# Products without a reader in the idle stretches of TensorE, first and last tile of an audio tower block

## The chip, the cores and the metric

The kernel runs on one core of one Trainium2 chip. The metric is the device time of one execution in microseconds, given as the median of the runs.

## The reference

The input x is 64 samples of 96 channels and 512 positions, fp32. First comes a small attention on each sample ("token attention"), then one transformer block (grouped attention, then a gated feed-forward with ternary weights) over the 64 x 32 rows of 512 that result:

```python
def reference(x, Wq, Wk, Wv, Wo, qn_w, kn_w, w1, w2, w3):
    q, k, v = split(x, 3, axis=1)                        # 64 x 32 x 512 each
    h = einsum('bts,bcs->bct', softmax(q^T k * scale), v)
    # attention of 16 query heads and 4 key/value heads of 128; rows of one sample
    # (32) attend to each other, causal; q and k are RMS-normed and rotated
    h = h + attn(layernorm(h), Wq, Wk, Wv, qn_w, kn_w) @ Wo.T
    y = layernorm(h)
    return h + (sigmoid(y @ Q(w1).T) * (y @ Q(w2).T)) @ Q(w3).T   # Q rounds to -1, 0, 1; 1408 hidden
```

## The kernel before

The program has two stages. `token_attention` computes the first attention and, beside it, prepares the weights in SBUF (fp16 high and low halves of the attention weights, `W.hi` and `W.lo`, and the ternary feed-forward weights). It ends near 390 us, and a barrier separates it from the second stage. `blocks`, the second stage, is the one that the diff touches.

`blocks` works on 16 tiles of 128 rows (`NTT`). Each engine has its own instruction stream, written out by hand; `over_tiles` gives it as `body(0)` (attention of tile 0 alone), a loop over tiles 1 to 14, `body(15)`, and `body(16)`, in which only the feed-forward of tile 15 is left. The loop body works on the attention of tile n and the feed-forward of tile n - 1 together. Engines wait for each other by semaphores that count upwards.

TensorE (the engine of the diff) issues in this order within a body:

- `project(n, c)` for c = 1 to 5 (lines 991 to 993): four column groups of Q, and V. The one of K, `project(n + 1, 0)`, is issued ahead, in the body before. Each has 12 products of 128x128 weights with 512 columns in fp16 (high x high, high x low, low x high, four slices of the depth). `project(n, 0)` waits for the transposed normalised rows `x_hi`, `x_lo`, which arrive by a DMA from what ScalarE and GpSimd write.
- `gate_products` (lines 1033, 1034) of the tile before: three groups (`FG`) by two halves, 176 products of 128 columns in all. The first waits for the second normalisation's rows, again by a transposing DMA.
- between them `transpose_qk` for c = 0 to 4 (line 985), at places that `TRANSPOSE_AT` lists. Each waits for `q_ready`, GpSimd's last step of the rotation and normalisation of that head group (`rope_sum`, lines 722, 725, 729). Then come the `scores` (line 1051, 32 small products), which wait for ScalarE's copies.
- `down_products` 0 to 3 (lines 1068, 1069), `project(n + 1, 0)`, `weigh_values` (line 1082, waits for the softmax that VectorE finishes in line 952), `down_products` 4 to 10, and `output_products` (lines 1096 to 1098, 48 products of 512 columns), which wait for the high and low halves of the context (`ctx_hi` by ScalarE, `ctx_lo` by VectorE, line 891).

In tile 0 there is no feed-forward, so TensorE has no gate and down products between the steps of the attention; in `body(15)` there is no next projection, and in `body(16)` nothing is left between the output products and the gate products but the second normalisation.

The eight PSUM banks are `PROJ[0..1]`, `TR[0..1]` and `FB[0..3]`. `FB[1..3]` hold projections or gate sums, and all four `FB` hold the context; `PROJ[1]` takes the output sum; `TR[0]` takes transposes and the down sum.

Of the kernel before, what the change touches and what calls it, by code (L numbers as in the profile page):

```python
# [16 lines left out]
P = 128  # L17
# [10 lines left out]
D = 512  # L28
# [3 lines left out]
Q_AT, K_AT, V_AT, O_AT = 0, KD * HEADS * HD, KD * (HEADS + KV) * HD, KD * (HEADS + 2 * KV) * HD  # L32
# [536 lines left out]
def blocks(nc, W, h1, tables_in, norm_in, mask_in, ident_in, out):  # L569

    with ExitStack() as ctx:
# [6 lines left out]
        PROJ = [ctx.enter_context(nc.psum_tensor(f"proj{n}", [P, D], FP32)) for n in range(2)]  # L578
        TR = [ctx.enter_context(nc.psum_tensor(f"transposed{n}", [P, D], FP32)) for n in range(2)]
        FB = [ctx.enter_context(nc.psum_tensor(f"ffn_sum{n}", [P, D], FP32)) for n in range(BT)]  # L580
# [70 lines left out]
        SCORES_AT = (1, 1)  # L651
        BANK = (PROJ[0], FB[2], FB[3], PROJ[0], PROJ[1], TR[1])
        DOWN_FIRST = 4
        block = ctx.enter_context(nc.Block())

        def over_tiles(eng, body):
# [322 lines left out]
        def _(pe):  # L979
            pe.wait_ge(const_in, 4 * DMA)  # L980

            def transpose(dst, src, last_sem):

                for k in range(KD):
                    t = nc.tensor.transpose(dst[:, k * P:(k + 1) * P], src[:, k * P:(k + 1) * P], ident[:, :])  # L985
                t.then_inc(last_sem, 1)

            def split_products(dst, pairs, done):

                for i, (ah, al, bh, bl) in enumerate(pairs):  # L990
                    nc.tensor.matmul(dst, ah, bh, start=(i == 0), stop=False)  # L991
                    nc.tensor.matmul(dst, ah, bl, start=False, stop=False)  # L992
                    t = nc.tensor.matmul(dst, al, bh, start=False, stop=(i == len(pairs) - 1))  # L993
                t.then_inc(done, 1)

            def project(n, c):

                if c == 0:
                    pe.wait_ge(x_turned, 2 * DMA * (n + 1))
                first = isinstance(n, int) and n == 0  # L1000
                if c == 0 and not first:
                    pe.wait_ge(squared, 5 * n - 1)
                    pe.wait_ge(roped_b, 5 * n - 1)
                if c == 3:
                    pe.wait_ge(squared, 5 * n + 1)
                    pe.wait_ge(roped_b, 5 * n + 1)
                if c in (1, 2) and not first:
                    pe.wait_ge(c_lo, BT * n)
                if c == 4 and not first:
                    pe.wait_ge(h2_done, n)  # L1010
                if c == NPROJ - 1 and not first:
                    pe.wait_ge(taken, n)
                pairs = []
                for k in range(KD):
                    at = (K_AT + k * KV * HD if c == 0 else V_AT + k * KV * HD if c == NPROJ - 1
                          else Q_AT + k * HEADS * HD + (c - 1) * D)
                    pairs.append((xh[:, k, :], xl[:, k, :], W.hi(at, D), W.lo(at, D)))
                split_products(BANK[c][:, :], pairs, proj)

            def gate_products(n, f, m):  # L1020

                if f == 0 and m == 0:
                    pe.wait_ge(x2_turned, 2 * DMA * (n + 1))
                    pe.wait_ge(c_hi, KV * (n + 1))
                    pe.wait_ge(c_lo, KV * (n + 1))
                if f == 2:
                    pe.wait_ge(gated, NF * n + 1 + START)
                for j, t in enumerate(FG[f]):
                    for k in range(KD):
                        at = (m * KD + k) * FF + t * P  # L1030
                        w = ffn_w[:, at:at + P]
                        dst = FB[2 * (f % 2) + m][:, j * P:(j + 1) * P]
                        nc.tensor.matmul(dst, w, x2h[:, k, :], start=(k == 0), stop=False)  # L1033
                        ins = nc.tensor.matmul(dst, w, x2l[:, k, :], start=False, stop=(k == KD - 1))  # L1034
                ins.then_inc(f1, 1)

            def transpose_qk(n, c, ffn):
                pe.wait_ge(q_ready, 5 * n + c + 1)
                if c == 0 and ffn:
                    pe.wait_ge(o_out, n - 1 + START)  # L1040
                if c == 1:
                    pe.wait_ge(v_out, n + 1)
                if c >= 2:
                    pe.wait_ge(qkt_out, 5 * n + c - 1)
                transpose(TR[c % 2], rope[:, c, :], qkt)

            def scores(n):
                pe.wait_ge(qkt_out, 5 * n + 5)
                for h in range(KV):
                    for b in range(BT):  # L1050
                        ins = nc.tensor.matmul(SCORES[b * SEQ:(b + 1) * SEQ, h * P:(h + 1) * P],
                                               kT[:, h, b * SEQ:(b + 1) * SEQ], qT[:, h, b * P:(b + 1) * P],
                                               start=True, stop=True)
                ins.then_inc(scored, 1)

            def down_products(n, tiles):
                if tiles[0] == 0:
                    if isinstance(n, int) and n + 1 >= NTT:
                        pe.wait_ge(o_out, n + START)
                    else:  # L1060
                        pe.wait_ge(qkt_out, 5 * (n + 1) + 5)
                for k in tiles:
                    if k == 0 or k in (FG[1][0], FG[2][0]):
                        f = [g[0] for g in FG].index(k)
                        pe.wait_ge(hid_hi, NF * n + f + 1)
                        pe.wait_ge(hid_lo, NF * n + f + 1)
                    at = 2 * KD * FF + k * D
                    nc.tensor.matmul(DOWN[:, :], hh[:, k, :], ffn_w[:, at:at + D], start=(k == 0), stop=False)
                    ins = nc.tensor.matmul(DOWN[:, :], hl[:, k, :], ffn_w[:, at:at + D], start=False,  # L1069
                                           stop=(k == KF - 1))  # L1070
                if tiles[-1] == KF - 1:
                    ins.then_inc(w3, 1)

            def weigh_values(n, ffn):
                pe.wait_ge(v_out, n + 1)
                pe.wait_ge(pt_out, n + 1)
                if ffn:
                    pe.wait_ge(gated, NF * n + START)
                for h in range(KV):
                    for b in range(BT):  # L1080
                        of = slice(b * SEQ, (b + 1) * SEQ)
                        ins = nc.tensor.matmul(FB[b][:, h * P:(h + 1) * P], v[of, h * HD:(h + 1) * HD], pT[of, h, :],  # L1082
                                               start=True, stop=True)
                ins.then_inc(pv, 1)

            def output_products(n):
# [11 lines left out]
                    ins = nc.tensor.matmul(PROJ[1][:, :], al, bh, start=False, stop=(k == HEADS - 1))  # L1098
                ins.then_inc(o_sum, 1)

            project(0, 0)

            def body(n, attn, ffn):
                last = isinstance(n, int) and n + 1 >= NTT
                if attn:
                    for c in range(1, NPROJ):
                        project(n, c)

                for f in range(NF):
                    for m in range(2):  # L1110
                        if ffn:
                            gate_products(n - 1, f, m)
                        if attn:
                            for c in TRANSPOSE_AT.get((f, m), []):
                                transpose_qk(n, c, ffn)
                            if (f, m) == SCORES_AT:
                                scores(n)
                if ffn:
                    down_products(n - 1, range(0, DOWN_FIRST))
                if attn and not last:  # L1120
                    project(n + 1, 0)
                if attn:
                    weigh_values(n, ffn)
                if ffn:
                    down_products(n - 1, range(DOWN_FIRST, KF))
                if attn:
                    output_products(n)

            over_tiles(pe, body)


def program(nc, qk, vt, w_attn, w_ffn, tables, norm_w, mask, ident, out):
    h1 = nc.dram_tensor("h1_rows", (TOK, D), FP32, kind="Internal").ap()
    with ExitStack() as ctx:
        W = Weights(lambda name, shape, dt=FP32: ctx.enter_context(nc.sbuf_tensor(name, shape, dt)))
        token_attention(nc, qk, vt, h1, ident, W, w_attn, w_ffn)
        blocks(nc, W, h1, tables, norm_w, mask, ident, out)
# [51 lines left out]
```

## Time and profile before

| what | value |
|---|---|
| median of 3 runs | 1162.64 us (1160.01 to 1163.67) |
| profiled execution | 1163.83 us |
| its span | 1161.7 us, mean granted TensorE clock 0.965 |
| TensorE matmul busy | 1078.6 us (93%) |
| VectorE, GpSimd, ScalarE busy | 721.7, 463.8, 419.9 us (62%, 40%, 36%) |
| chain that ended last | 55% TensorE, 3% VectorE, 2% GpSimd |

The span runs from the first to the last instruction; the execution's own time is 2.1 us longer. Busy shares are averages over both stages. A matmul's row gives its start and its full duration, but matmuls overlap: the distance from one start to the next is what one costs in a row of them. The granted clock is a share of TensorE's full speed, 1.00 for 2.4 GHz and 0.50 for 1.2 GHz.

### The profile page before, as it was taken

The page shows a single profiled execution, that of the slowest core. Times are in us where ns is not written, and L with a number is a line of the kernel's source. Part 1 is how long each engine was busy: PE and PEld are TensorE (multiplying, and loading weights), DVE is VectorE, ACT ScalarE, POOL GpSimd, SP SyncE. Part 2 cuts the span into 40 slices and gives each one's busy share as a digit, 9 for nine tenths or more (in the row PEclk, how much of TensorE's full clock was granted, in tenths as well). Part 3 has the DMA queues.
Part 4 walks back from the last instruction along what each step waited for, and adds up shares of the span by engine and source line. Part 5 has one row for each costly group of instructions (what it writes and reads, how often), then busy time and mean ns, then how long its engine had stood idle before and what let it go on. Part 6 is the DMA issues. An engine that isn't in the chain of part 4 may idle for free.

```text
span 1161.7 us, 21798 instructions
## 1 busy us (share of the span) xinstructions
PE 1078.6 (93%) x8640; PEld 592.2 (51%) x8640; DVE 721.7 (62%) x1277; ACT 419.9 (36%) x733; POOL 463.8 (40%) x350
## 2 busy tenths in 40 slices
PE   4999989889999478999999999999999999999996
PEld 2434333443333234664665755646646656557554
DVE  6687765766687165665755765765656557557642
ACT  1666555545556221332321412323323314223221
POOL 2001026665556263452451552543534524615410
PEclk9999998889999689999999999999999999999998
DMA  6988844554442200110101010110111010110100
GB/s 183 311 311 267 301 117 126 150 180 126 142 124 79 67 19 19 29 27 31 30 21 36 18 36 27 27 36 27 27 36 27 20 34 18 36 36 18 28 11 19
DMA packets 70584, 92.21 MB, mean 79 GB/s; under 512 B 39312, under 2 KB 40080, under 8 KB 70544
## 3 DMA queue, kind: packets, MB, share of 16 engines
q1 hardware_dynamic: 70544, 91.66, 26.5%
q8 instruction: 27, 0.44, 0.2%
q14 instruction: 13, 0.11, 0.0%
HBM read 49.43 MB, written 8.39 MB: 50 GB/s over the span
## 4 chain that ended last, share of the span: by engine, by line
PE 55%; issue 4%; DVE 3%; POOL 2%; ACT 1%; DMA 1%; SPq 0%; POOLq 0%; DVEq 0%
PE ffn_sum L1033 7%; PE ffn_sum L1034 6%; PE proj L1096 5%; PE proj L1098 4%; PE proj L1097 4%; PE proj L991 3%; PE proj L993 3%; PE proj L992 3%; PE transposed L985 3%; DVE ctx_lo L891 2%; PE ffn_sum L993 2%; PE ffn_sum L991 2%; PE ffn_sum L992 2%; PE ffn_sum L1082 2%; PE transposed L1069 1%
## 5 line engine op out<-in xcount | busy, mean ns | idle before, releaser
L334 DVE TENSOR_REDUCE row_max<-score_rows 128x1 f32<-128x512 f32 x256 | 167.1, 685 | 91.1 <-PE score_rows L474 89.6
L722 POOL TENSOR_TENSOR roped<-rope_cos,rope_sin 128x512 f32<-128x512 f32 x80 | 101.5, 1269 | 249.7 <-DVE rope_sin L860 249.7
L293 ACT ACTIVATE exps<-score_cols 128x512 f32<-128x512 f32 x256 | 146.1, 601 | 136.0 <-PE score_cols L499 133.9
L1033 PE MATMUL ffn_sum<-x_hi,ffn_w 128*128 128x128 f16 x1408 | 167.8, 221 | 7.7 <-DMA x_lo<-x_lo_rows 7.7
L1034 PE MATMUL ffn_sum<-x_lo,ffn_w 128*128 128x128 f16 x1408 | 167.6, 221 | 0.0
L1033 PEld LDWEIGHTS ffn_sum<-x_hi,ffn_w 128*128 128x128 f16 x1408 | 138.6, 99 | 12.9 <-DMA x_lo<-x_lo_rows 8.2
L474 PE MATMUL score_rows<-k_parts,q_parts 96*128 96x512 f32 x256 | 125.6, 504 | 16.2 <-DMA k_parts<-qk_low 14.9
L1034 PEld LDWEIGHTS ffn_sum<-x_lo,ffn_w 128*128 128x128 f16 x1408 | 138.9, 99 | 2.3
L474 PEld LDWEIGHTS score_rows<-k_parts,q_parts 96*128 96x128 f32 x256 | 52.7, 207 | 130.4 <-DVE row_max L334 72.4
L499 PE MATMUL score_cols<-q_parts,k_parts 98*128 98x512 f32 x256 | 108.6, 430 | 10.5 <-DMA q_parts<-max_t 6.2
L1096 PE MATMUL proj<-attn_slots,ctx_hi 128*128 128x512 f16 x256 | 97.5, 381 | 5.9 <-DVE ctx_lo L891 5.9
L1098 PE MATMUL proj<-attn_slots,ctx_lo 128*128 128x512 f16 x256 | 97.5, 381 | 0.0
L1097 PE MATMUL proj<-attn_slots,ctx_hi 128*128 128x512 f16 x256 | 97.5, 381 | 0.0
L763 ACT ACTIVATE squares<-ffn_sum 128x512 f32<-128x512 f32 x32 | 19.0, 594 | 214.1 <-PE ffn_sum L993 214.1
L248 POOL TENSOR_TENSOR qk_low<-qk_raw,qk_high 128x1024 fp32r<-128x1024 f32 x16 | 38.9, 2429 | 143.7 <-ACT qk_high L287 143.7
L729 POOL TENSOR_TENSOR roped<-roped,rms_inv 128x512 f32<-128x512 f32 x80 | 86.3, 1078 | 11.5
L991 PE MATMUL proj<-attn_slots,x_hi 128*128 128x512 f16 x192 | 74.7, 389 | 15.9 <-DMA x_lo<-x_lo_rows 15.9
L971 DVE SCALAR_TENSOR_TENSOR h<-proj,o_unscale,h_res 128x512 f32<-128x512 f32 x16 | 12.0, 750 | 122.5 <-PE proj L1098 122.5
L725 POOL TENSOR_TENSOR rms_inv<-mean_sq,minus_half 128x4 f32<-128x4 f32 x80 | 85.1, 1063 | 4.8
L718 POOL TENSOR_TENSOR rstd<-var,minus_half 128x1 f32<-128x1 f32 x32 | 25.0, 782 | 148.8 <-DVE var L838 148.8
L992 PE MATMUL proj<-attn_slots,x_hi 128*128 128x512 f16 x192 | 74.8, 390 | 0.0
L993 PE MATMUL proj<-attn_slots,x_lo 128*128 128x512 f16 x192 | 74.8, 390 | 0.0
(120 smaller groups left out, 2004.5 us busy)
## 6 DMA issues: line engine op xcount, KB each, us to landing
raw_ffn<-in_w_ffn SPq DMA_DIRECT2D x24, 704.0 KB, 7.3
attn_slots<-in_w_attn SPq DMA_DIRECT2D x20, 512.0 KB, 11.1
qk_raw<-in_qk SPq DMA_DIRECT2D x16, 512.0 KB, 5.8
q_parts<-qk_high SPq DMA_DIRECT2D x32, 256.0 KB, 3.3
k_parts<-qk_high SPq DMA_DIRECT2D x32, 256.0 KB, 4.4
v_t<-in_v_t SPq DMA_DIRECT2D x16, 256.0 KB, 5.7
q_parts<-qk_low SPq DMA_DIRECT2D x16, 256.0 KB, 4.9
k_parts<-qk_low SPq DMA_DIRECT2D x16, 256.0 KB, 5.2
```

What stands on the lines that cost most here:

```text
L293: nc.scalar.activation(E[:, (STEPS * g + u) % NE, :], ST[(STEPS * g + u) % 3][:, :], ACT.Exp, scale=TOK_SCALE).then_inc(exp_done, 1)
L334: nc.vector.reduce_max(row_max[:, g % 2, k:k + 1], S[n % NS][:, :], AX.X).then_inc(s_free, 1)
L474: nc.tensor.matmul(bank[:, :], QP[g % NB][0:3 * CH, b, t * P:(t + 1) * P], KP[g % NB][0:3 * CH, b, :], start=True, stop=True).then_inc(s_f ...
L499: nc.tensor.matmul(ST[n % 3][:, :], KP[g % NB][0:3 * CH + 2, b, i * P:(i + 1) * P], QP[g % NB][0:3 * CH + 2, b, :], start=True, stop=True) ...
L991: nc.tensor.matmul(dst, ah, bh, start=(i == 0), stop=False)
L992: nc.tensor.matmul(dst, ah, bl, start=False, stop=False)
L993: t = nc.tensor.matmul(dst, al, bh, start=False, stop=(i == len(pairs) - 1))
L1033: nc.tensor.matmul(dst, w, x2h[:, k, :], start=(k == 0), stop=False)
L1034: ins = nc.tensor.matmul(dst, w, x2l[:, k, :], start=False, stop=(k == KD - 1))
L1096: nc.tensor.matmul(PROJ[1][:, :], ah, bh, start=(k == 0), stop=False)
L1097: nc.tensor.matmul(PROJ[1][:, :], ah, bl, start=False, stop=False)
L1098: ins = nc.tensor.matmul(PROJ[1][:, :], al, bh, start=False, stop=(k == HEADS - 1))
```

## The change

A function `keep_busy(bank, count)` issues `count` products of 128x128 fp16 weights with 512 fp16 columns into a PSUM bank. They read two slices of the attention weights that lie in SBUF, wait for nothing, signal nothing, and no engine reads what they write. They stand at six kinds of places: 10 before the first projection of tile 0; in tile 0 4, 11 and 2 before the transposes of head groups 2, 3 and 4, 8 before the K projection of tile 1, and 12 before the output products; 9 before the last tile's `weigh_values`; and 32 before the gate products of the tail. That is 88 products. The loop over tiles 1 to 14 has none.

```diff
--- before.py
+++ after.py
@@ -651,6 +651,7 @@
         SCORES_AT = (1, 1)
         BANK = (PROJ[0], FB[2], FB[3], PROJ[0], PROJ[1], TR[1])
         DOWN_FIRST = 4
+        WAITS = {2: 4, 3: 11, 4: 2}
         block = ctx.enter_context(nc.Block())
 
         def over_tiles(eng, body):
@@ -1098,29 +1099,46 @@
                     ins = nc.tensor.matmul(PROJ[1][:, :], al, bh, start=False, stop=(k == HEADS - 1))
                 ins.then_inc(o_sum, 1)
 
+            def keep_busy(bank, count):
+
+                for _ in range(count):
+                    nc.tensor.matmul(bank[:, :], W.hi(K_AT, P), W.hi(Q_AT, D), start=True, stop=True)
+
+            keep_busy(FB[0], 10)
             project(0, 0)
 
             def body(n, attn, ffn):
+                first = isinstance(n, int) and n == 0
                 last = isinstance(n, int) and n + 1 >= NTT
                 if attn:
                     for c in range(1, NPROJ):
                         project(n, c)
 
+                if not attn:
+                    keep_busy(FB[2], 32)
                 for f in range(NF):
                     for m in range(2):
                         if ffn:
                             gate_products(n - 1, f, m)
                         if attn:
                             for c in TRANSPOSE_AT.get((f, m), []):
+                                if first and c >= 2:
+                                    keep_busy(FB[0], WAITS[c])
                                 transpose_qk(n, c, ffn)
                             if (f, m) == SCORES_AT:
                                 scores(n)
                 if ffn:
                     down_products(n - 1, range(0, DOWN_FIRST))
+                if first:
+                    keep_busy(FB[0], 8)
                 if attn and not last:
                     project(n + 1, 0)
+                if last and attn:
+                    keep_busy(PROJ[0], 9)
                 if attn:
                     weigh_values(n, ffn)
+                if first:
+                    keep_busy(TR[0], 12)
                 if ffn:
                     down_products(n - 1, range(DOWN_FIRST, KF))
                 if attn:
```

## Rows read from the trace of the kernel before

**Rows 1.** The page: granted TensorE clock in 40 slices of the span, tenths.

```profile
PEclk9999998889999689999999999999999999999998
```

**Rows 2.** Windows over stretches of the block stage: busy time by engine, granted clock (PEclk).

```profile
400.20:405.40 5.20, 5.14 (x13) 1.81 (x14) 0.00 (x0) 0.00 (x0) 0.00 (x0) 0.50 0.32 103
430.40:435.80 5.40, 5.31 (x16) 1.73 (x16) 3.03 (x5) 0.63 (x1) 0.00 (x0) 0.50 0.16 52
440.40:452.00 11.60, 11.56 (x48) 5.06 (x49) 2.48 (x5) 0.00 (x0) 3.33 (x3) 0.89 0.00 0
465.00:1087.00 622.00, 619.39 (x5569) 379.61 (x5568) 388.11 (x736) 180.18 (x331) 267.69 (x246) 1.00 0.11 28
1118.90:1122.20 3.30, 3.30 (x9) 1.13 (x8) 2.48 (x4) 1.72 (x4) 0.00 (x0) 0.50 0.00 0
1141.40:1146.10 4.70, 4.70 (x45) 4.70 (x46) 0.00 (x0) 0.60 (x1) 0.00 (x0) 0.50 0.00 0
```

**Rows 3.** The timeline of TensorE, tile 0 and start of tile 1: start, us, what, idle before.

```profile
400.26 0.59 PE L991 MATMUL proj<-attn_slots,x_hi 128*128 128x512 f16 x1 [13.60 <-DMA x_lo<-x_lo_rows]
...
405.34 0.47 PE L991 MATMUL ffn_sum<-attn_slots,x_hi 128*128 128x512 f16 x1
...
419.32 1.10 PE L985 MATMUL transposed<-ident,roped 128*128 128x128 f32 x8 [0.34 <-ACT v L801]
421.52 0.65 PE L985 MATMUL transposed<-ident,roped 128*128 128x128 f32 x4 [1.09 <-POOL roped L729]
424.90 0.66 PE L985 MATMUL transposed<-ident,roped 128*128 128x128 f32 x4 [2.73 <-POOL roped L729]
426.23 1.94 PE L1051 MATMUL transposed<-q_t,k_t 128*32 128x128 f32 x32 [0.68 <-ACT q_t L784]
430.49 0.61 PE L991 MATMUL proj<-attn_slots,x_hi 128*128 128x512 f16 x1 [2.32 <-DMA x_lo<-x_lo_rows]
...
435.72 1.40 PE L1082 MATMUL ffn_sum<-probs_t,v 32*128 32x128 f32 x32
440.44 0.59 PE L1096 MATMUL proj<-attn_slots,ctx_hi 128*128 128x512 f16 x1 [3.32 <-DVE ctx_lo L891]
...
452.08 0.38 PE L991 MATMUL ffn_sum<-attn_slots,x_hi 128*128 128x512 f16 x1
...
465.03 0.22 PE L1033 MATMUL ffn_sum<-x_hi,ffn_w 128*128 128x128 f16 x1
...
466.81 1.04 PE L985 MATMUL transposed<-ident,roped 128*128 128x128 f32 x8
```

**Rows 4.** The chain that ended last, at the start of the block stage.

```profile
391.63 2.82 DMA ident<-in_identity
```

**Rows 5.** The timeline of GpSimd in tile 0.

```profile
407.71 1.27 POOL L722 TENSOR_TENSOR roped<-rope_cos,rope_sin 128x512 f32<-128x512 f32 x1 [10.20 <-DVE rope_sin L860]
```

**Rows 6.** The timeline of VectorE, last step of the softmax, first and last tile.

```profile
433.62 0.71 DVE L952 STREAM_TRANSPOSE probs_t<-probs 128x512 f32<-128x512 f32 x1
...
1116.52 0.71 DVE L952 STREAM_TRANSPOSE probs_t<-probs 128x512 f32<-128x512 f32 x1
```

**Rows 7.** The timeline of TensorE, tiles 14 and 15 and the tail.

```profile
1072.17 1.17 PE L1082 MATMUL ffn_sum<-probs_t,v 32*128 32x128 f32 x32
...
1076.66 0.38 PE L1096 MATMUL proj<-attn_slots,ctx_hi 128*128 128x512 f16 x1 [0.19 <-DVE ctx_lo L891]
...
1109.41 1.08 PE L1051 MATMUL transposed<-q_t,k_t 128*32 128x128 f32 x32
...
1117.33 1.17 PE L1082 MATMUL ffn_sum<-probs_t,v 32*128 32x128 f32 x32 [2.33 <-issue]
...
1123.16 0.38 PE L1096 MATMUL proj<-attn_slots,ctx_hi 128*128 128x512 f16 x1
...
1141.39 0.29 PE L1033 MATMUL ffn_sum<-x_hi,ffn_w 128*128 128x128 f16 x1 [7.71 <-DMA x_lo<-x_lo_rows]
...
1153.51 0.38 PE L1068 MATMUL transposed<-ffn_w,hidden_hi 128*128 128x512 f16 x1
```

## The prediction

> **What bounds the kernel now.** I read the page's clock line first [rows 1]: TensorE is granted full clock in most of the 40 slices of 29 us. Slices 7 to 9 show 8, but they lie in the token stage, which the diff leaves alone; slice 14 shows 6, slice 15 shows 8, and so does the last one. Slices 14 and 15 (378 to 436 us) are where the token stage hands over to the block stage. Next come the windows [rows 2]. From 465 to 1087 us TensorE is busy 619.39 of 622 us at clock 1.00 (its 2.4 GHz level): tiles 1 to 14 are bound by TensorE and nothing in them is touched. Four other windows show clock 0.50 (1.2 GHz), and that from 440.40 to 452.00 a mean of 0.89, which is (1 - 0.89) x 11.6 / 0.5 = 2.6 us at 0.50 and then 1.00. They are: the first products of tile 0 (400.2), the projection of tile 1's K (430.4), the start of the output products (440.4), the last tile's down products (1118.9) and the tail's gate products (1141.4). Each follows a stretch in which TensorE did little: 13.60 us idle before 400.26, 2.32 before 430.49, 3.32 before 440.44 [rows 3], 2.33 before 1117.33 and 7.71 before 1141.39 [rows 7]. So the end is set by a line of waits through tile 0, then TensorE, then a tail; products at the lower clock lie on that line wherever nothing else is later.
>
> **What a product costs at either level.** Between 452.08 and 465.03 lie the 60 products of five projections [rows 3]: 12.95 / 60 = 0.216 us each, 128x512 fp16. The 12 from 400.26 to 405.34 took 5.08, so 0.423 each. An added product has that same shape and type (128x128 weights, 512 columns, fp16), so I price it at 0.216 with the clock up and 0.423 with it down; these are both bounds. It waits for nothing and signals nothing. It delays a real product only if the group outlasts the idle time that it is put in. The banks are ones whose last readers TensorE has already been made to wait for, or is never refilled before them, so no wait is added.
>
> **The edits, one by one.** All times are those of before, before any shift.
>
> *Ten in front of the first projection.* TensorE passes its wait for the constants when the last of four DMAs lands, 391.63 + 2.82 = 394.45 [rows 4]. Ten at the lower clock take 4.23, to 398.7; the first product waits for a DMA until 400.26, so there are 1.6 us to spare even at the lower clock. If they raise the clock and it stays up over that 1.6 us, the 12 products take 12 x 0.216 = 2.59 and not 5.08: 2.49. Is that on the path? GpSimd's first rope addition at 407.71 had been idle 10.20 us for VectorE [rows 5], which waits for these products; its work then runs without a pause, and releases the transposes at 421.52 and at 424.90 [rows 3], 3.38 us apart, one per head group. So all of tile 0 starts earlier. The next projections take 2.59 each, under GpSimd's 3.38 per step, so TensorE is not late next. **2.49 us.**
>
> *Four, eleven and two in front of three transposes.* The third group of transposes is the second half of the eight that start at 419.32 and take 1.10 with the last one's tail (an estimate: 0.44 a group without it), so it starts at 419.76. With four ahead: 419.76 + 0.86 = 420.62, its own 0.44, eleven 2.38, to 423.4; the group that was released at 421.52 is thus 1.9 us late, then its own 0.44 and two more, 0.43, to 424.3. The last group is released only at 424.90: 0.6 us to spare, and ScalarE's copy of the late one (0.6 us) also ends before it. The delay is hidden by GpSimd; without that cover it would cost 1.9. In return TensorE is no longer nearly idle from 422 to 424.9. The scores (32 small products at 426.23, 1.94 us in the timeline at 0.50) should take the 1.08 us that they take in the last tile at full clock [rows 7]; the path behind them is priced in the next part.
>
> *Eight in front of tile 1's K projection.* The scores then end at 427.2, eight end at 427.2 + 1.73 = 428.97, and the x_lo transpose releases the projection at 430.49: 1.5 us to spare. The 12 products end at 430.49 + 2.59 = 433.08, not at 435.6. What is late next is the softmax: its last VectorE step ends at 433.62 + 0.71 = 434.33 [rows 6], and 0.86 earlier behind faster scores, 433.47. In the last tile the product behind it started 0.10 after it (1117.23 to 1117.33) [rows 6, 7], so weighing starts at 433.57 instead of 435.72. **2.15 us**, and only 1.29 if the scores stay slow.
>
> *Twelve in front of the output products.* From weighing to the first output product it is 4.72 in tile 0 (435.72 to 440.44) and 4.49 at full clock (1072.17 to 1076.66) [rows 3, 7]: **0.23**. Twelve take 2.59 behind weighing's 1.17, so 0.73 are left of 4.49. The 48 output products took 452.08 - 440.44 = 11.64 and at 0.216 take 10.36: **1.28 us**.
>
> *Nine in front of the last weighing.* The gap is 2.33 (TensorE waits for the softmax), nine take 1.94: 0.4 to spare. The clock fell at 1118.9 for 3.3 us [rows 2] because of that gap. Down products then end before the context halves are there, so the output products start at 1117.33 + 4.49 = 1121.82 and not 1123.16 [rows 7]. **1.34 us.**
>
> *Thirty-two in front of the tail.* 48 output products from 1123.16 end at 1133.52; 32 x 0.216 = 6.91, to 1140.4; the DMA releases the gate products at 1141.39, so 1.0 to spare. The 176 gate products took 1153.51 - 1141.39 = 12.12 [rows 7]. At full clock 32 of them take 466.81 - 465.03 = 1.78 [rows 3], so 176 take 9.80. **2.32 us.** VectorE and ScalarE behind them had idle time and move along.
>
> **The sum.** 2.49 + 2.15 + 0.23 + 1.28 + 1.34 + 2.32 = 9.81 us. It is made against the profiled execution, 1163.83 (span 1161.7), so 1154.0. That execution lies 1.2 above the median of the runs, 1162.64. I take that difference as the low-clock stretches falling differently in each run (before spreads over 3.7 us), and since the change removes just those, I do not subtract it again: 1154.0 is both.
>
> **What is unknown is the clock.** In this trace the granted clock rose 5.1 us after the first product at 400.26 (0.50 over that whole window), and 2.6 us after the one at 440.44 [rows 2], though TensorE had just been idle: the delay is not fixed. So ten products over 4.2 us may or may not raise it, and it may fall again in the 1.6 us pause. The bounds for the first edit are 0 and 2.49; I take 2.49, since ten and then twelve are far more than what raised it at 440.44.
> The Trainium skill, "TensorE: Matmul & The Clock Gate", Part 1, says that the throttle is the default and activity releases it, and that what watches the activity runs freely, so that the same kernel shows a different count of slow products from run to run. The two different delays here agree. By that rule the first group sometimes fails: then the sum is 7.3 and not 9.8.
>
> **Rivals.**
> *A. The first group does not help (or the clock falls again in its pause).* 1163.83 - 7.32 = 1156.5. For it: at 400.26 the clock took 5.1 us of unbroken products to rise, and the ten are 4.2. Against: at 440.44 it took 2.6. Chance 0.2.
> *B. Groups overshoot or one more of the later stretches stays slow.* The smallest reserves are 0.4, 0.6 and 0.73 us; weighing and scores are small products and one of them also preceded a fall at 1118.9. One of the terms 1.28, 1.34, 2.15 or 2.32 is lost besides A's, or a group at the lower clock overshoots by 1 to 2 us: 1157.8 to 1160. Chance 0.1.
> *C. No effect.* The granted clock does not follow such products, or a stretch that I think is on the path is hidden: 1162.6. Against: the stretches at 0.50 all follow idle time, and tiles 1 to 14, which have none, show no fall. Chance 0.05.
> *D. Slower: the added products themselves run at the lower clock.* Then the 17 before the transposes take 7.19 + 0.88 from 419.76, to 427.8 against 424.90 (2.9 late); the eight make 3.4 against 2.3 free (1.1); the twelve 5.08 + 1.4 against 4.72 (1.8); the nine 3.81 against 2.33 (1.5); and the 32 13.5 against 7.87 (5.7). Together 13.0 later, 1176.8. It decides if most groups run low; the 32 alone at that level would eat 5.7 + 2.32 of the gain and give 1162.0. Against it: each of these groups but the first follows products at full clock. Chance 0.03.
>
> **How the numbers follow.** My forecast has 0.62, A 0.2, B 0.1, C 0.05, D 0.03. A measurement of this kernel can tell 0.3%, 3.5 us, from no change: under 1159.15 is faster. The forecast, A and most of B are there: 0.90. Within 0.3%: C, the rest of B, and the half of D in which only the tail runs low, 0.08. Slower 0.02. The range goes from 1152.0 (all terms, and a share of the 1.2 us below the profiled run) to 1158.5, which takes in A and the nearer half of B and leaves out about 0.15.
>
> **What would show it.** Right: clock 1.00 from the first projection to the end; the first twelve products in 2.6 us; scores in 1.1; idle times before the same waiting lines (400.26, 430.49, 440.44, 1141.39) shortened by the added products but still above zero; 48 output products in 10.4 and 176 gate products in 9.8; tiles 1 to 14 unchanged at their period. Wrong: an added group followed at once by the real product that used to be released by a DMA, VectorE or GpSimd (overshoot), or a stretch at 0.50 behind an added group. The prediction fails as a whole if the clock ignores these products, or if GpSimd's rope chain does not move with the first projection.

## The result, and the profile after

The changed kernel takes 1158.83 us (median of 11 runs, 1153.25 to 1160.8) against 1162.88 for the kernel before in the same runs: a ratio of 0.996, 95% interval 0.9943 to 0.9977. It is faster, as forecast, but by 4.05 us where the sum gave 9.8, and the median lies 0.3 us above the upper end of the range. The ratio, applied to the 1162.64 from which the prediction started, gives 1158.0, just inside it. The profiled execution took 1160.36 us, its span is 1158.1.

The page of the kernel after, granted clock by slice, answers to [rows 1]:

```profile
PEclk9999998899989799999999999999999999999999
```

The last slice shows 9 where it showed 8, and slice 14 shows 7 instead of 6. The windows of the block stage, which answer to [rows 2] (columns as there):

```profile
396.70:401.20 4.50, 4.42 (x10) 1.34 (x10) 1.15 (x2) 0.62 (x1) 1.15 (x1) 0.50 0.16 33
401.20:402.40 1.20, 0.02 (x1) 0.00 (x0) 0.00 (x0) 0.00 (x0) 0.00 (x0) 0.50 0.54 108
402.40:405.80 3.40, 3.34 (x8) 1.19 (x9) 0.00 (x0) 0.00 (x0) 0.00 (x0) 0.50 0.52 154
406.10:433.20 27.10, 23.30 (x143) 11.71 (x142) 17.14 (x35) 7.55 (x13) 17.96 (x17) 1.00 0.07 12
433.40:436.60 3.20, 3.20 (x9) 1.10 (x8) 1.36 (x2) 0.00 (x0) 0.00 (x0) 0.50 0.16 58
436.80:1155.50 718.70, 713.39 (x6352) 434.44 (x6350) 435.41 (x823) 201.53 (x370) 292.74 (x269) 1.00 0.11 27
```

The clock is at 1.00 from 436.80 to the end, as predicted, and from 406.10 to 433.20. But the first added products (396.70) run at 0.50, the clock is still at 0.50 after them, over most of the first projection (402.40), and it falls again for 3.4 us at 433.3, in the middle of tile 1's K projection. The timeline of TensorE, which answers to [rows 3, 7]:

```profile
396.78 4.45 PE L1105 MATMUL ffn_sum<-attn_slots 128*128 128x512 f16 x10 [8.15 <-DMA ident<-in_identity]
402.46 0.61 PE L992 MATMUL proj<-attn_slots,x_hi 128*128 128x512 f16 x1 [1.23 <-DMA x_lo<-x_lo_rows]
...
406.76 0.38 PE L992 MATMUL ffn_sum<-attn_slots,x_hi 128*128 128x512 f16 x1
...
426.28 0.66 PE L986 MATMUL transposed<-ident,roped 128*128 128x128 f32 x4 [0.46 <-POOL roped L730]
427.61 1.08 PE L1052 MATMUL transposed<-q_t,k_t 128*32 128x128 f32 x32 [0.67 <-ACT q_t L785]
428.63 1.90 PE L1105 MATMUL ffn_sum<-attn_slots 128*128 128x512 f16 x8
432.85 0.39 PE L992 MATMUL proj<-attn_slots,x_hi 128*128 128x512 f16 x1 [2.33 <-DMA x_lo<-x_lo_rows]
...
437.23 1.17 PE L1083 MATMUL ffn_sum<-probs_t,v 32*128 32x128 f32 x32
438.34 2.76 PE L1105 MATMUL transposed<-attn_slots 128*128 128x512 f16 x12
441.72 0.38 PE L1097 MATMUL proj<-attn_slots,ctx_hi 128*128 128x512 f16 x1 [0.62 <-DVE ctx_lo L892]
...
1132.23 7.07 PE L1105 MATMUL ffn_sum<-attn_slots 128*128 128x512 f16 x32
1140.11 0.23 PE L1034 MATMUL ffn_sum<-x_hi,ffn_w 128*128 128x128 f16 x1 [0.81 <-DMA x_lo<-x_lo_rows]
```

Ten added products begin at 396.78, when the constants have landed, and 1.23 us of idle time follow them; the first projection takes 406.76 - 402.46 = 4.30. Eight begin at 428.63, but the projection behind them starts only at 432.85, after 2.33 us of idle time. The groups of twelve (438.34) and of 32 (1132.23) fill their gaps, with 0.62 and 0.81 left. The constants land at 396.73 here and at 394.45 before: 2.3 us of the token stage and of the loads behind it, which the change does not touch. Piece by piece (in us; "last transposes" is the fifth group, [rows 3] 424.90; the first projection of each kernel starts 5.7 to 5.8 behind the constants):

| stretch | before | predicted | after |
|---|---|---|---|
| first projection (12 products) | 5.08 | 2.59 | 4.30 |
| scores | 1.94 | 1.08 | 1.08 |
| last transposes to weighing, tile 0 | 10.82 | 8.67 | 10.95 |
| weighing to output products | 4.72 | 4.49 | 4.49 |
| 48 output products | 11.64 | 10.36 | 10.36 |
| last tile, weighing to output products | 5.83 | 4.49 | 4.55 |
| 176 gate products | 12.12 | 9.80 | 9.83 |
| constants landed to end of span | 767.25 | | 761.37 |

The block stage is 5.9 us shorter in this execution. The terms 0.23, 1.28, 1.34 and 2.32 came out within 0.1; what is missing are 1.7 of the first and the whole 2.15 of the second.

**Why the second was missing.** SyncE issues the transposing DMAs of `x_hi` and `x_lo`, which release the K projection. Its timeline before, and then after:

```profile
426.72 1.20 SPq L682 DMA_TRANSPOSE x_hi<-x_hi_rows  x1
427.97 1.26 SPq L684 DMA_TRANSPOSE x_lo<-x_lo_rows  x1
```

```profile
428.11 2.17 SPq L683 DMA_TRANSPOSE x_hi<-x_hi_rows  x1
430.32 1.26 SPq L685 DMA_TRANSPOSE x_lo<-x_lo_rows  x1
```

The issue of `x_hi` took 2.17 us instead of 1.20, so `x_lo` went out a microsecond late and the projection started 6.57 after the last transposes instead of 5.59. In the DMA view of the kernel after, 427.5 to 430 us, there is one packet of the instruction queue q8 (packets, MB, share of 16 engines). I take that queue to be TensorE's, because its packets move when TensorE's instructions are moved (experiment 5):

```profile
q8 instruction: 1, 0.02, 2.8%
```

In the kernel before there is none between 426 and 430. The 27 products that stand ahead of the scores, and the eight behind them, move TensorE's instruction stream by two instructions each (a weight load and a matmul), and with it the place where its next 16 KB are fetched (the page's queue view: 28 packets, 0.46 MB).

All twelve profiles of this document bear this out. From 386 us to the end they hold some 1400 DMA issues of SyncE. Twenty-two took clearly longer than others of their kind (transposing 1.43 to 2.22 us instead of 1.20 to 1.32, plain 1.23 to 1.95 instead of 0.3 to 0.6), and a packet of q8 overlaps every one of them. Eighteen more issues are touched by a packet and keep their usual time, among them all four transposing ones that the packet reached more than 0.8 us after their start. One long issue from the kernel of experiment 4, with the packet in the DMA view of 471.5 to 473.7 us, where no product was added nearby:

```profile
470.31 1.19 SPq L683 DMA_TRANSPOSE x_hi<-x_hi_rows  x1
471.55 2.04 SPq L685 DMA_TRANSPOSE x_lo<-x_lo_rows  x1
...
q8 instruction: 1, 0.02, 3.1%
```

### The profile page after: what moved, and what is told of

Its sections match the earlier page's. It is cut to its first block, busy times and chain, and to the rows that moved or that the text cites. A ratio compares the mean times of both kernels' runs of the same rounds, so it can differ in the third digit from the quotient of the medians.

```text
span 1158.1 us, 21973 instructions
## 1 busy us (share of the span) xinstructions
PE 1094.4 (94%) x8728; PEld 597.4 (52%) x8728; DVE 722.3 (62%) x1277; ACT 420.1 (36%) x733; POOL 463.4 (40%) x350
## 4 chain that ended last, share of the span: by engine, by line
PE 54%; issue 4%; DVE 3%; POOL 2%; ACT 1%; DMA 1%; SPq 1%; POOLq 0%; DVEq 0%
PE ffn_sum L1034 7%; PE ffn_sum L1035 6%; PE proj L1097 5%; PE proj L1099 4%; PE proj L1098 4%; PE proj L992 3%; PE proj L993 3%; PE proj L994 3%; PE transposed L986 3%; DVE ctx_lo L892 2%; PE ffn_sum L994 2%; PE ffn_sum L992 2%; PE ffn_sum L993 2%; PE ffn_sum L1083 1%; PE transposed L1070 1%
## 5 line engine op out<-in xcount | busy, mean ns | idle before, releaser
L730 POOL TENSOR_TENSOR roped<-roped,rms_inv 128x512 f32<-128x512 f32 x80 | 86.3, 1078 | 11.5
```

## The experiments

All are timed in the same way; ratios are to the kernel before, timed beside each, with 95% intervals. For each kernel there is one profile. Since the token stage ends at a different time in each execution (below), the text compares stretches of the profiles as well: "block stage" is from the landing of the constants to the end of the span.

**1. Without the first ten.**

```diff
-            keep_busy(FB[0], 10)
             project(0, 0)
```

> The changed kernel without its first group of ten products. In the profile of the changed kernel these ten did not have the clock up when the first projection began; that projection took 4.30 us, against 5.08 before. Theory 1 (the ten are too few to raise the clock every time, and then lie idle for 1.2 us): the first projection takes 4 to 5.1 us here as well, and the median is within 1.5 us of the changed kernel's 1158.8. Rival (the ten bring their 2.49 us in most runs, and the profile caught one of the others): the median is 2 us or more above it, 1161.

1159.65 us, ratio 0.9984 (0.9962 to 1.0005): the interval overlaps with that of the changed kernel, so the medians do not tell what the ten give. The first projection took 4.97, the block stage 761.90, 0.5 more than with the ten. The ten are worth less than a microsecond in this pair. Over all profiles with ten in that place the first projection took 4.30, 4.28, 4.28 and 2.60; without any, 5.08, 4.97, 4.80, 5.05 and 4.58.

**2. Only the 32 of the tail.**

```diff
-            keep_busy(FB[0], 10)                 # and the groups of 4, 11, 2, 8, 9 and 12
                 if not attn:
                     keep_busy(FB[2], 32)
```

> The kernel before with the 32 products in front of the tail's gate products as the only group. Theory 1 (the groups act one by one, through the clock alone): 176 gate products in 9.8 us where they took 12.12, clock 1.00 up to them, 2.3 us off the part from the output products of the last tile to the end; median near 1160.5. Rival (groups only work together, or most of the measured 4 us is not the clock of the block stage): gate products still above 11 us, or a median as before, 1162.9.

1161.66 us, ratio 1.0002 (0.9986 to 1.0017). In the profile the 176 gate products take 9.83 as in the full change, so the group works alone; the time as a whole does not show the expected 2.3: the interval of the ratio allows a gain of 1.6 us at most. What the 32 save also depends on the execution: in the three profiles without products in that place the gate products took 12.12 (before), 11.31 (experiment 5) and 11.91 (experiment 10), so the saving is 1.5 to 2.3. This profile also shows the last tile without the nine:

```profile
1116.48 1.17 PE L1083 MATMUL ffn_sum<-probs_t,v 32*128 32x128 f32 x32 [2.33 <-issue]
...
1121.03 0.38 PE L1097 MATMUL proj<-attn_slots,ctx_hi 128*128 128x512 f16 x1 [0.25 <-DVE ctx_lo L892]
```

TensorE idles 2.33 ahead of weighing, exactly as before, but the output products follow after 4.55, not 5.83: the clock did not fall.

**3. Sixteen in the tail.**

```diff
-                    keep_busy(FB[2], 32)
+                    keep_busy(FB[2], 16)
```

> The changed kernel with 16 instead of 32 products in front of the gate products: they end 3.5 us after the output products and TensorE then stands idle for about 4.3 us. Theory 1 (a pause of that length lets the clock fall whatever came ahead of it): clock 0.50 at the first gate products, 176 of them in 11.5 to 12.2 us, 2 us slower than the changed kernel. Rival (half the products keep most of the clock): gate products in 9.8 to 10.5 us and no difference.

```profile
1132.23 3.62 PE L1105 MATMUL ffn_sum<-attn_slots 128*128 128x512 f16 x16
1140.11 0.29 PE L1034 MATMUL ffn_sum<-x_hi,ffn_w 128*128 128x128 f16 x1 [4.26 <-DMA x_lo<-x_lo_rows]
...
1135.90:1140.10 4.20, 0.00 (x0) 0.00 (x0) 0.69 (x1) 0.39 (x1) 0.00 (x0) 0.97 0.31 62
1140.20:1143.20 3.00, 3.00 (x30) 3.00 (x31) 0.00 (x0) 0.00 (x0) 0.00 (x0) 0.50 0.00 0
```

4.26 us idle are left; the clock is up over nearly all of it (mean 0.97) and at 0.50 when the gate products begin. These take 11.32 instead of 9.83, so 1.5 of the 2.3 is gone. Even the other 0.8 is not shown to be the sixteen's doing, since the kernel of experiment 5, with no product there, took 11.31. The median, 1159.29, ratio 0.9987 (0.9962 to 1.0012), differs from the changed kernel's by too little to tell. The size expected (11.5 to 12.2) was a little high.

**4. Sixty-four in the tail.**

```diff
-                    keep_busy(FB[2], 32)
+                    keep_busy(FB[2], 64)
```

> The changed kernel with 64 instead of 32 in the tail. At 0.216 each they take 13.8 us in a gap of 7.9. Theory 1 (a product that overshoots costs its full 0.216 and nothing hides it): the first gate product starts 13.8 us after the last output product and with no idle time ahead of it, 5.9 us later than in the changed kernel (which waits 7.9 us); the median is 5.9 us above the changed kernel's, 1164.7, slower than the kernel before. Rival (TensorE drops or overlaps what no one reads): less than 2 us.

```profile
1128.02 13.98 PE L1105 MATMUL ffn_sum<-attn_slots 128*128 128x512 f16 x64
1141.83 0.22 PE L1034 MATMUL ffn_sum<-x_hi,ffn_w 128*128 128x128 f16 x1
```

1141.83 - 1128.02 = 13.81 for 64, 0.216 each, and nothing idle in front of the gate products, which start 5.94 later after the first output product than in the changed kernel (24.17 against 18.23). Median 1163.64, ratio 1.0008 (0.9992 to 1.0023): the overshoot eats the gain of the whole change. So an added product that overshoots costs what a real one does, and the 32 had to fit.

**5. The kernel before, with its instruction stream moved.** 40 products of 32 columns ahead of the wait for the constants:

```diff
+            for _ in range(40):
+                nc.tensor.matmul(FB[0][:, 0:32], W.hi(K_AT, P), W.hi(Q_AT, 32), start=True, stop=True)
             pe.wait_ge(const_in, 4 * DMA)
```

> The kernel before with 40 added products of only 32 columns at the start of the block stage, 1 to 2 us of work in a stretch where TensorE waits 4 us for constants. They do nothing for the clock; they only move TensorE's instruction stream by 80 instructions. In every profile so far that has the added products ahead of the scores, a 16 KB packet of the instruction queue q8 lands while SyncE issues tile 1's transposing DMA of x_hi, and that issue takes 1.99 to 2.22 us instead of 1.20; in the two without, the packet comes later and the issue takes 1.20. Theory 1 (the instruction fetch makes the issue longer): the packet moves into 426 to 428 us (in the time of before), the issue takes 2.0 to 2.2 here too, and the K projection of tile 1 starts 6.4 to 6.6 us after the last transposes and not 5.6. Rival (TensorE's faster scores or its added products slow the issue): 1.20 and 5.6, as before.

1165.45 us, ratio 1.0037 (1.0017 to 1.0057): slower than before, though the 40 take 1.2 us that were idle. SyncE in the profile, first at the constants and then at tile 1's transposing DMAs, with the instruction packet of the DMA view of 426 to 429:

```profile
389.25 0.42 SPq L678 DMA_DIRECT2D norm_w<-in_norm_weights  x1
389.72 1.95 SPq L678 DMA_DIRECT2D mask<-in_causal  x1
391.71 0.43 SPq L678 DMA_DIRECT2D ident<-in_identity  x1
...
426.49 1.20 SPq L682 DMA_TRANSPOSE x_hi<-x_hi_rows  x1
427.73 2.01 SPq L684 DMA_TRANSPOSE x_lo<-x_lo_rows  x1
...
q8 instruction: 1, 0.02, 2.7%
```

The packet did move into this place. It lengthened the issue of `x_lo` (2.01 instead of 1.26) and not that of `x_hi`, which I had named; the K projection started 6.48 after the last transposes, as expected, and weighing 11.22 after them (before 10.82). And a second meeting that I had not foreseen: TensorE now begins instructions while SyncE issues the loads of the constants, and the issue of the mask took 1.95 instead of 0.43. From SyncE's store of the last token rows to the landing of the constants it is 8.7 us here, and 7.0 before. These two delays are what the profile has to offer for the slower median, but they do not prove its cause. The profiled execution, 1160.31, was one of the fastest of the twelve; its block stage is 763.45, 3.8 shorter than in before's profile, since less of it ran at 0.50 (first projection 4.58, output products 10.36, last tile 4.55, gate products 11.31).

**6. The changed kernel, moved by the same 40.**

```diff
+            for _ in range(40):
+                nc.tensor.matmul(FB[0][:, 0:32], W.hi(K_AT, P), W.hi(Q_AT, 32), start=True, stop=True)
             pe.wait_ge(const_in, 4 * DMA)
...
             keep_busy(FB[0], 10)
```

> The changed kernel with the same 40 narrow products ahead of it. Theory 1: the instruction packet comes earlier, before the scores, the issue of x_hi falls back to 1.20 us, the K projection starts 5.6 us after the last transposes, TensorE's pause ahead of it shrinks from 2.3 to 1.4 us, and the clock stays up through it: weighing starts 8.7 us after the last transposes instead of 10.95. Block stage from the landing of the constants to the end: 759 us instead of 761.4, median 1 to 2.5 us below the changed kernel's. Rival (the issue time has another cause): 2.2 us and 10.4 to 10.95 again.

1156.48 us, ratio 0.9955 (0.9936 to 0.9973).

```profile
430.58 1.20 SPq L683 DMA_TRANSPOSE x_hi<-x_hi_rows  x1
431.82 1.26 SPq L685 DMA_TRANSPOSE x_lo<-x_lo_rows  x1
...
428.75 0.66 PE L988 MATMUL transposed<-ident,roped 128*128 128x128 f32 x4 [0.46 <-POOL roped L730]
...
434.36 0.39 PE L994 MATMUL proj<-attn_slots,x_hi 128*128 128x512 f16 x1 [1.36 <-DMA x_lo<-x_lo_rows]
...
437.48 1.17 PE L1085 MATMUL ffn_sum<-probs_t,v 32*128 32x128 f32 x32 [0.36 <-DVE probs_t L953]
```

`x_hi` is issued in 1.20, the pause is 1.36, the clock stays up, and weighing starts 437.48 - 428.75 = 8.73 after the last transposes: the 8.67 of the prediction, where the changed kernel took 10.95. The block stage is 759.47, 1.9 shorter than the changed kernel's.

That gain does not reach the end. The constants landed 8.8 us after the store instead of 7.3 in the changed kernel: the last load took 4.59 us from its issue to its landing, where the eleven other profiles have 2.7 to 3.3. Its issue kept its 0.43, but a q8 packet lies in the DMA view of 394.6 to 396. From the chain that ended last:

```profile
394.64 4.59 DMA ident<-in_identity
```

From the store to the end it is 768.3 against 768.7, and the ratios 0.9955 and 0.996 cannot be told apart.

**7. Busy through the hand-over.**

```diff
-            pe.wait_ge(const_in, 4 * DMA)
-            keep_busy(FB[0], 10)
+            keep_busy(FB[0], 14)       # and 14 of 32 columns
+            pe.wait_ge(const_in, 4 * DMA)
+            keep_busy(FB[0], 22)
...
-                    keep_busy(FB[0], 8)
+                    keep_busy(FB[0], 13)
```

> The changed kernel with TensorE kept busy through the whole hand-over: 14 wide and 14 narrow products ahead of the wait for the constants (about 390 to 396 us in the time of before), 22 wide ones behind it instead of 10, and 13 instead of 8 ahead of tile 1's K projection. Theory 1 (the ten fail because they are short and a pause follows them): the first projection takes 2.6 us in the profile and in nearly every run, x_hi is issued in 1.20 us, weighing starts 8.7 us after the last transposes; block stage 757.5 to 758 us, median near 1155.5. Rival (with a clock that rises when it likes, more products only overshoot): first projection above 4 us, or it starts more than 5.9 us after the constants.

1155.3 us, ratio 0.9954 (0.9936 to 0.9973). First projection 2.60, weighing after 8.73, block stage 757.43, all as expected. But the issue of the mask took 1.61, and the constants landed 1.3 us late, measured from the store (8.3 against 7.0).

**8. Fifteen behind the constants.**

```diff
-        WAITS = {2: 4, 3: 11, 4: 2}
+        WAITS = {2: 2, 3: 9, 4: 2}    # and 14 of 32 columns each for 2 and 3
...
-            keep_busy(FB[0], 10)
+            keep_busy(FB[0], 15)
...
-                    keep_busy(FB[0], 8)
+                    keep_busy(FB[0], 13)
```

> The changed kernel with 15 instead of 10 products behind the constants, 13 instead of 8 ahead of tile 1's K projection, and in front of the transposes of head groups 2 and 3 two wide products each replaced by 14 of 32 columns (same time, 24 more instructions each). Nothing runs ahead of the wait for the constants, since in the two kernels with products there an issue of a constant's load took 1.61 and 1.95 us instead of 0.43 and the constants landed 1.3 to 1.8 us later. Theory 1: first projection in 2.6 us, starting at most 0.3 later than 5.7 behind the constants; the issue of x_hi 1.20; weighing 8.7 us after the last transposes; from SyncE's store of the token stage's last rows to the end 764 us (changed kernel: 768.7, handover kernel: 765.8); median 1154. Rival (the clock rises late and the fifteen overshoot, or the instruction packet still meets the transposing DMA): 767 or more.

1154.39 us, ratio 0.9929 (0.9912 to 0.9947): the lowest median of all, its interval hardly overlapping with the changed kernel's. From experiments 7 and 9 it cannot be told apart.

```profile
391.61 5.50 PE L1105 MATMUL ffn_sum<-attn_slots 128*128 128x512 f16 x15 [7.72 <-DMA ident<-in_identity]
397.29 0.39 PE L992 MATMUL proj<-attn_slots,x_hi 128*128 128x512 f16 x1 [0.18 <-DMA x_lo<-x_lo_rows]
...
425.02 0.39 PE L992 MATMUL proj<-attn_slots,x_hi 128*128 128x512 f16 x1 [0.27 <-DMA x_lo<-x_lo_rows]
...
428.15 1.06 PE L1083 MATMUL ffn_sum<-probs_t,v 32*128 32x128 f32 x28 [0.37 <-DVE probs_t L953]
...
421.25 1.20 SPq L683 DMA_TRANSPOSE x_hi<-x_hi_rows  x1
```

The fifteen end 0.18 us ahead of the first projection, which takes 2.60; thirteen leave 0.27 ahead of the K projection. From the store to the end it is 764.4 (before 774.3, after 768.7). The block stage is 757.44: 9.8 under before's profile, the sum of the prediction, once all of its terms are really there. Experiments 7 and 9 have the same block stage (757.43 and 757.48). How much of the 9.8 a median shows depends on how slow the block stage of before happens to be.

**9. Started by the first rows.**

```diff
-            pe.wait_ge(const_in, 4 * DMA)
-            keep_busy(FB[0], 10)
+            pe.wait_ge(ln_in, DMA)
+            keep_busy(FB[0], 18)       # and 22 of 32 columns
+            pe.wait_ge(const_in, 4 * DMA)
...
-                    keep_busy(FB[0], 8)
+                    keep_busy(FB[0], 13)
```

> The changed kernel with TensorE waiting for the first rows (which land after SyncE has issued all loads of constants, and 1.8 us ahead of the last constant), then 18 wide and 22 narrow products, then the wait for the constants; and 13 products instead of 8 ahead of tile 1's K projection. Theory 1: products start at 392.7 in the time of before, the constants' issues take 0.43 each, the first projection starts 5.7 to 6 us after the constants land and takes 2.6, x_hi is issued in 1.20 and weighing starts 8.7 after the last transposes; 763.7 to 764 us from the store to the end, median 1154, with less spread than the changed kernel's 7.5 us. Rival: an instruction packet meets a transfer on the path here too, 765 or more.

1155.29 us, ratio 0.993 (0.9906 to 0.9954), a spread of 8.5 us, not less than the changed kernel's, so that part of the expectation fell. The profile is as expected: constants' issues 0.43 each, first projection 2.58, block stage 757.48, 764.8 from the store. It also answers a question that experiment 8 leaves open, whether the ten failed for being too short or for the pause behind them (windows: columns as in [rows 2]):

```profile
401.07 0.71 PE L1108 MATMUL ffn_sum<-attn_slots 128*128 128x32 f16 x22
403.24 0.38 PE L990 MATMUL proj<-attn_slots,x_hi 128*128 128x512 f16 x1 [1.46 <-DMA x_lo<-x_lo_rows]
...
395.20:401.00 5.80, 5.77 (x18) 2.27 (x19) 2.18 (x5) 0.62 (x1) 1.75 (x2) 0.65 0.30 85
401.80:403.20 1.40, 0.00 (x0) 0.00 (x0) 0.00 (x0) 0.00 (x0) 0.00 (x0) 1.00 0.50 100
```

The clock rose while the eighteen ran and stayed at 1.00 through 1.46 us of idle time, longer than the pause behind the ten. So in this profile a pause of that length did no harm once the clock was up.

**10. Only the nine of the last tile.**

```diff
                 if last and attn:
                     keep_busy(PROJ[0], 9)   # the other groups left out
```

> The kernel before with the nine products in front of the last weighing as the only group. Two profiles without the nine (the tail-alone kernel has none there, and the kernel with 40 narrow products none at all) showed 4.55 us from weighing to the output products, against 5.83 in the kernel before, whose profile had the clock fall there. Theory 1 (the fall is a matter of where the granted clock happened to be, and the prediction counted it as always there): 4.55 us, and a median within 1 us of before's, 1161.9 to 1162.6, less than the 1.34 us of the prediction; the low-clock stretches in tile 0 and in the tail differ from those of before's profile by up to 3 us in sum. Rival (the fall is the rule and those two were exceptions): median 1.3 us below before, 1161.2.

1162.05 us, ratio 0.9991 (0.9973 to 1.0008): no difference that can be told, but the interval still allows a gain of 1.3 us, so the median does not decide between the two theories. 4.55 us from weighing to the output products, as in the two profiles that had no products there. In tile 0 its 48 output products took 13.28, where before's profile shows 11.64, and that of the 40 narrow products alone 10.36.

## Why the prediction was right or wrong

*Right: what the groups do.* A product costs 0.216 and delays nothing while it fits; 64 in place of 32 cost 5.94 as worked out. The clock follows such products, so rival C is out, and in the kernel as changed all groups but the first ran at 1.00 and none overshot, so D is out. The scores, weighing, output and gate products of the profile after came within 0.1 of the sum. GpSimd hid the late transposes: from the end of the first projection to the last transposes it is 19.56 before and 19.52 after. And tile 1 to the last weighing is 665.25 in both.

*Wrong, the first step: "I take 2.49".* The ten run while the clock is low, end 1.2 us ahead of the projection, and gave about 0.8 in three of four profiles and all of it in one (2.60, experiment 4, where the clock rose in the pause). This is rival A, which I gave 0.2, in three of four profiles. My argument compared ten products with what had raised the clock at 440.44, though before's clock was at 0.99 from 436.2 to 439.4 and had fallen no more than 1.1 us ahead of them. The Trainium skill, "TensorE: Matmul & The Clock Gate", Part 1, has the count of slow products vary from run to run of one kernel; the four profiles, of kernels that have the same ten products there, agree (4.30, 4.28, 4.28 and 2.60). The pause is not what failed: in experiment 9 the clock stayed up through a longer one. In the three kernels with longer groups (experiments 7 to 9) the clock rose while the group still ran, and the first projection took 2.60, 2.60 and 2.58.

*Wrong, the second step: "the x_lo transpose releases the projection at 430.49: 1.5 us to spare".* I moved no DMA in my sum, but the change moves TensorE's instruction fetch. Its packet met the issue of the transposing DMA, the pause grew to 2.33, the clock fell 0.4 us after it, and 2.15 became -0.13. In number this is my rival B, one of the later terms lost besides A's, which I gave 0.1; its cause was in none of my rivals. Experiments 5 and 6 show the late issue from both sides: moving the stream alone brings it into the kernel before, and takes it out of the changed kernel, whose profile then shows the 2.2. The fall goes with the length of the pause: of the eight kernels with products ahead of the K projection, the four with 2.1 to 2.4 us of idle time there had the clock fall early in it, the four with 0.3 to 1.4 us did not. The length alone does not decide it, for in the last tile the same 2.33 us was followed by a fall in one profile and by none in two. Why a packet lengthens an issue stays open.

*Wrong in size: the sum was made against one execution.* The 1.34 of the last tile was counted as always there. Of the three profiles without products in that gap two took 4.55 and only one 5.83, and experiment 10 shows no gain that can be told. The 2.32 of the tail was likewise taken from the slowest of three such profiles (12.12, 11.91, 11.31). The low-clock stretches in tile 0 go both ways (48 output products: 10.36, 11.64, 13.21, 13.28), so the block stage of before is not one number.

*Wrong: where the runs' spread comes from.* I took the 1.2 us between the profiled execution and the median as low-clock stretches of the block stage. But SyncE's store at the end of the token stage, which no edit touches, starts between 382.7 and 390.4 us in the twelve profiles. That alone is wider than the spread that I wanted to explain, and it is a likely reason, not a proven one, why kernels whose profiles differ by 2 us here can't be told apart by a median.

In numbers: less A (1.7) and the lost second term (2.3), 9.8 becomes 5.8, and the profile shows 5.9; the median of 4.05 is lower still, and a last tile that loses its 1.34 only in some executions, and a tail that loses 1.5 to 2.3, go that way. That the time came out at the edge of the range is partly luck: the lower half of the gain was in the range for rival A's sake, and a delay that I had not thought of took the result just to its end. How much each of the terms holds in the median stays open, since one profile for each kernel was taken.

## What to carry to other kernels

Where an engine's clock follows its activity, filling idle time pays what the next real work loses at the low clock, and only if the clock is up when that work begins. Ten products, which ended at the low clock, gave a third of the gain in three of four profiles; longer groups, which still ran when the clock rose, gave all of it in three of three, one of them with a pause of 1.46 us behind it. Leave a reserve, since every product too many costs its full time. Read such stretches in several profiles before you sum them: some were there in every profile here, with a length that varies, and others only in some. And when instructions are added, look where the instruction queue's packets fall afterwards, above all against DMA issues that something waits for.

## What the runs showed of the hardware

- A 16 KB packet of the instruction queue q8 that overlaps an issue of SyncE can lengthen it: transposing DMAs 1.43 to 2.22 us instead of 1.20 to 1.32, plain ones 1.23 to 1.95 instead of 0.3 to 0.6. All 22 long issues in twelve profiles are such; 18 others that a packet touches kept their time.
- 40 products of 32 columns, which move the instructions behind them, made the kernel before slower, 1.0037 (1.0017 to 1.0057). Its profile shows two issues lengthened by packets; that they are the whole cause is not shown.
- With 4.26 us of idle time the granted clock stayed at 1.00 for nearly all of it (mean 0.97) and was down when the work began: idle time itself shows 1.00 in the windows, and the price appears only behind it.
